# Taking the constant products out of TensorE's waits in a four-layer decoder kernel

## The reference

```python
x = x + _L0_attn_ref(_layernorm(x, axis=-1), ...)
x = x + _L0_xattn_ref(_layernorm(x, axis=-1), ctx_1024, ...)
x = x + _L0_ffn_ref(_layernorm(x, axis=-1), ...)
...
x = x + _L3_ffn_ref(_layernorm(x, axis=-1), ...)
```

## Time and profile before

| | |
|---|---|
| median of three runs | 1903.01 us |
| lowest and highest | 1902.84 and 1909.08 us |
| profiled execution | 1902.77 us |
| its span from first to last instruction | 1901.0 us |
| TensorE busy (matmul) | 1667.9 us, 88% |
| VectorE, ScalarE, GpSimd busy | 62%, 48%, 24% |
| mean granted TensorE clock | 0.952 of full |

### The profile page before, as it was taken

How to read it: one execution, slowest core, us unless ns; L and a number is a source line. 1 busy time by engine, 2 the same in 40 slices (tenths; PEclk the granted TensorE clock), 3 DMA queues, 4 the chain that set the end, 5 groups by cost and what they waited for, 6 DMA issues and landing times. The chain is left out here.

```text
span 1901.0 us, 37141 instructions
## 1 busy us (share of the span) xinstructions
PE 1667.9 (88%) x13775; PEld 1293.5 (68%) x13778; DVE 1177.0 (62%) x2317; ACT 921.2 (48%) x1953; POOL 449.8 (24%) x501
## 2 busy tenths in 40 slices
PE   7978855789999799976878879999999988999898
PEld 4766733558888646643667647777777766888676
DVE  3676688656666612226545678888888865666622
ACT  2445576246666411111344456767676644555432
POOL 1020011023333032221300224545445530000200
PEclk9999977899999999998989989999999989999899
DMA  2020000300010172221000000101010112110000
GB/s 101 3 92 3 4 30 27 118 18 26 25 33 25 68 317 44 46 50 38 15 2 28 18 17 26 33 25 33 25 33 25 28 39 100 34 33 25 1 1 22
DMA packets 27679, 77.58 MB, mean 41 GB/s; under 512 B 2992, under 2 KB 14896, under 8 KB 25392
## 3 DMA queue, kind: packets, MB, share of 16 engines
q1 hardware_dynamic: 23488, 70.91, 10.9%
q0 software_dynamic: 4080, 5.13, 1.7%
HBM read 62.75 MB, written 13.28 MB: 40 GB/s over the span
## 5 line engine op out<-in xcount | busy, mean ns | idle before, releaser
L2575 DVE SCALAR_TENSOR_TENSOR arena<-bank,arena 128x508 f32<-128x508 f32 (+2 forms) x204 | 151.5, 743 | 27.9 <-ACT arena L2571 15.6
L2701 PE MATMUL bank<-L3a_wo,L3a_y_gated 128*128 128x256 f32 x512 | 124.0, 386 | 0.0
L2930 DVE TENSOR_TENSOR L3a_decays<-L3a_decays,L3a_cb_masked 128x512 f32<-128x512 f32 x128 | 94.7, 802 | 43.4 <-ACT L3a_decays L2813 43.4
L225 PE MATMUL bank<-const 128*128 128x512 f32 (+1 forms) x156 | 79.6, 644 | 42.5 <-PEq L65 42.5
L2813 ACT ACTIVATE L3a_decays<-bank 128x512 f32<-128x512 f32 x128 | 66.1, 602 | 97.0 <-PE bank L2675 97.0
L2728 PE MATMUL bank<-L3a_xnT_high,L3a_w_high 128*128 128x512 f32 x256 | 105.8, 413 | 1.5 <-ACT L3a_decays L2813 1.5
L2701 PEld LDWEIGHTS bank<-L3a_wo,L3a_y_gated 128*128 128x128 f32 x512 | 92.4, 190 | 17.6 <-issue 7.3
L2728 PE MATMUL bank<-L3a_xnT_high,L3a_w_low 128*128 128x512 f32 x256 | 99.8, 390 | 0.0
L2728 PE MATMUL bank<-L3a_xnT_low,L3a_w_high 128*128 128x512 f32 x256 | 99.7, 389 | 0.0
L1932 PE MATMUL bank<-L1f_experts,xnT 128*128 x184 | 84.6, 604 | 0.9 <-DVE xnT L2035 0.7
L3027 POOL TENSOR_TENSOR arena<-arena 128x1024 f32<-128x1024 f32 x32 | 81.3, 2541 | 14.7 <-ACT arena L2820 14.7
(11 more groups left out here) (612 smaller groups left out, 4641.2 us busy)
## 6 DMA issues: line engine op xcount, KB each, us to landing
arena<-in_L3p SPq DMA_DIRECT2D x32, 388.0 KB, 3.0
L1f_experts<-in_L1f SPq DMA_DIRECT2D x8, 1536.0 KB, 19.7
arena<-in_L1x SPq DMA_DIRECT2D x18, 384.0 KB, 3.0
arena<-in_L3x SPq DMA_DIRECT2D x18, 384.0 KB, 3.0
arena<-in_L0f SPq DMA_DIRECT2D x1, 4224.0 KB, 13.2
arena<-in_L3f SPq DMA_DIRECT2D x1, 4055.0 KB, 12.3
rows_sent<-L1a_blank SPq DMA_DIRECT2D x1, 2967.0 KB, 11.2
xnT<-rows_sent SPq DMA_DIRECT2D x23, 129.0 KB, 2.0
```

The costliest lines, as they stand in the source:

```text
L225: self.nc.tensor.matmul(self.k.ps[bank][:, 0:width], self.k.ident, self.k.const[:, 0:width], start=True, stop=True)
L2575: return nc.vector.scalar_tensor_tensor(dst[:, :, d:], psum[:, :, 0:P - d], wcol, dst[:, :, d:], ALU.mult, ALU.add)
L2701: mm = nc.tensor.matmul(ps[g // 2][:, (g % 2) * C:(g % 2 + 1) * C], yg[:, o, g * P:(g + 1) * P], wo[:, o, :], start=False, stop=False, ski ...
L2930: nc.vector.tensor_tensor(d, d, cbm[:, 4 * half:4 * half + 4, :].rearrange("p b t -> p (b t)"), ALU.mult).then_inc(S["dec_ready"], 1)
```

## The change

All calls of `idle` and the function itself are removed; the waits, the transposes and all other instructions stay as they are.

```diff
-    def idle(self, pe, n, width=HALF, bank=7):
-
-        for _ in range(n):
-            self.nc.tensor.matmul(self.k.ps[bank][:, 0:width], self.k.ident, self.k.const[:, 0:width], start=True,
-                                  stop=True)
-
     def tensor(self, pe):
         nc, k = self.nc, self.k
-        if self.busy:
-            self.idle(pe, 2)
         for h in range(2):
             for j in range(4):
                 b = 4 * h + j
                 by_dve = b in self.BY_DVE
-                if self.busy and b in ((1, 2) if self.measured else (1, 2, 3, 5, 6, 7)):
-                    self.idle(pe, 1, C)
                 pe.wait_ge(self.s_xn[by_dve], (self.BY_DVE if by_dve else self.BY_ACT).index(b) + 1)
...
                 r.matmuls(gate_w)
-                ln.idle(pe, 6, bank=6)
                 pe.wait_ge(s_both, 1)
...
                 mm.then_inc(s_prefix, 1)
-                ln.idle(pe, BUSY, bank=7)
                 pe.wait_ge(s_owner, 1)
```

More of the change, by code:

```diff
@@ L3514 @@
 CENTRED = 6 * C
-TILES, BUSY, ROW = 23, 28, C + 2
+TILES, ROW = 23, C + 2
 STAGES = [l0_attn, l0_xattn, l0_ffn, l1_attn, l1_xattn, l1_ffn, l2_attn, l2_xattn, l2_ffn, l3_attn, l3_xattn, l3_ffn]
```

## The result

| | before | changed |
|---|---|---|
| median of 11 runs each | 1904.04 us | 1912.97 us |
| lowest to highest | 1900.01 to 1909.08 us | 1908.9 to 1916.76 us |
| span of the profiled execution | 1901.0 us | 1908.3 us |
| mean granted clock | 0.952 | 0.929 |

The account below looks back on a forecast made before the run. Most stages were taken to run at TensorE's pace (88% busy). Earlier transposes -3.8, dense matmuls +10.4, narrow +9.6, router +0.4 gave +16.6 us; less 4 us for spared places, +12.6 us: 1915.5 us, range 1899 to 1926 us.

Parts of the forecast that it names:

- within 0.5%: Whole kernel: time within 0.5%, 9.5 us, of the kernel before, chance 0.40; slower than that got 0.56.
- hidden or half paid: Rival, chance 0.35: later waits absorb late first matmuls, or the low clock lasts 2 us, not 4; +6.6 us, 1909 us.
- Price of the low clock: Stage starts at 1.2 GHz: 32 narrow matmuls cost 3.2 us more, 16 transposes take 3.4 us, dense matmuls cost double.
- Term 4: Router of l1_ffn: prefix sums start 1.9 us earlier, run 1.8 us slower, first expert tile loses 0.5 us; +0.4 us.
- two places in ten are spared: Ten stage starts: transposes alone raise the clock in two, taking 4 us off, from +16.6 to +12.6 us.
- terms 2 and 3: Stage starts: first matmuls run at 1.2 GHz, dense ones costing +10.4 us and narrow ones +9.6 us.
- Term 3: l1_ffn, l2_ffn and l3_attn: 32 narrow first matmuls at 1.2 GHz cost 3.2 us each stage, +9.6 us.
- the low clock feeds on itself: Rival, chance 0.12: after narrow matmuls the clock stays at 1.2 GHz for denser ones; three places at 3 us more, 1924 us.
- The clock at 1.00 at the first matmul in most stages: Sign at the stage starts that the prediction is wrong and the kernel gets faster instead.
- the faster case: Rival, chance 0.06: constants are mostly delay, transposes raise the clock in nearly every stage; about -10 us, 1893 us.
- The gap interrupts it, so I let it start anew: Stage starts: the 0.7 us copy gap restarts the clock's rise; 4 us at 1.2 GHz from first matmul, 2 us lost.
- The mean clock: Sign over the whole kernel: mean granted clock falls from 0.952 to about 0.94, some 35 us more at the low level.

Follow-up runs that it names:

- router_out: Kernel before without only the 34 router constants in l1_ffn, the stage starts keeping theirs: 1904.01 us against 1904.19, ratio 0.9998.
- combined: Kernel before with start constants kept in three stages, one product at other starts, one in the gaps, none at the router: 1902.44 us against 1901.12, ratio 1.0002.
- the second profile: The changed kernel run once more, unaltered, for another trace: one execution, 1914.79 us, on a chip where the kernel before has a median of 1901.12 us.
- gap_filled: Changed kernel plus one 256-column constant product behind the last transpose in nine stages: 1907.65 us against 1904.19 for the kernel before, ratio 1.0004.
- front_filled: Changed kernel plus one 256-column constant product ahead of the first transpose in nine stages: 1914.4 us against 1904.84 for the kernel before, ratio 1.0046.
- l3a_out: Kernel before without the constants in l3_attn alone: 1905.95 us against 1904.84, ratio 1.0009.

## Why the prediction was right, and where it was off

The sign held, and the mechanism in part: the kernel is slower because the clock is at 1.2 GHz behind some stage starts, but in fewer of them than forecast, at a higher price in two, and in one (`l2_ffn`) not at the first matmul. The chip gave +8.9 us where the forecast was +12.5 us, so the time came out inside the range, and by the prediction's own bound it lies on the side called "within 0.5%" (0.47%), to which 0.40 was given and not 0.56. The rival "hidden or half paid", +6.6 us, is nearer to it than the forecast.

- *Price of the low clock.* 32 narrow matmuls: forecast 3.60 + 3.2 = 6.8 us, measured 6.88 us. Sixteen transposes: forecast 3.4 us and 0.4 to drain, measured 3.81 us; the first matmul 0.3 us earlier in `l2_attn`, measured, from ScalarE's root, 5.92 us in place of 6.21, 0.3 us. For `l3_ffn` forecast 1.4 us earlier, measured 5.80 in place of 7.30, 1.5 us. These prices were right.
- *Term 4.* The prefix sums gained 1.8 us and lost 1.9 us to the clock. Forecast +0.4 us, and `router_out` measured nothing to tell from it.
- *The step that was off* is "two places in ten are spared". In the changed kernel's trace the clock was up at the first matmul in six of the ten starts: in `l1_xattn`, for about 1 us, as forecast, and in `l0_attn`, `l1_ffn`, `l2_attn`, `l2_ffn` and `l3_ffn`, for which terms 2 and 3 had 12.4 us in all. Taking these off by the prediction's own prices leaves +4.2 us. The profiles differ by 7.4 us because, for the most part, other entries were too small: `l1_attn` and `l3_attn` cost 7.9 us and not 5.7, `l1_ffn` and `l2_ffn` together 2.7 us and not -0.2. That these errors offset each other to land inside the range is partly luck.
- *Term 3 was too large in two of its three stages.* It priced the 32 narrow matmuls at 0.2 us each in all three. In `l1_ffn` and `l2_ffn` they started at 2.4 GHz and the clock fell on the way, 4.81 and 4.73 us in place of 3.71, about 1 us more each and not 3.2; only in `l3_attn` was it 3.3 us. There, too, the narrow matmuls left the clock low and the dense ones behind them began at 1.2 GHz (4.43 us in all). That is the case called "the low clock feeds on itself", in one stage. `l2_ffn` before, then changed:

```profile
1044.46 3.71 PE L302 MATMUL bank<-arena,xnT 128*128 128x6 f32 x32 [0.72 <-ACT xnT L219]
...
1046.89 4.73 PE L292 MATMUL bank<-arena,xnT 128*128 128x6 f32 x32 [0.72 <-ACT xnT L219]
```

- *A sign that misled.* "The clock at 1.00 at the first matmul in most stages" was to mean the faster case. It came, six in ten, and the kernel is slower all the same: two stages at 0.50 outweigh the rest.
- *Hidden lateness.* `l2_xattn` was not spared, yet lost 0.33 us, not 1.7. Three traces in which the clock fell 0.9 us ahead of its first transpose separate this from luck: it stayed low for 3.4 us in the kernel before, 6.8 us in `combined` and 10.2 us in the changed kernel, and the stage took 118.20, 118.20 and 118.53 us. So the low clock is taken up later in the stage; which wait takes it up I did not look for. (Where the clock fell at another moment, as in the second profile, the stage is 2.0 to 2.5 us shorter.)
- *The gap.* "The gap interrupts it, so I let it start anew" was an assumption. `gap_filled` against `front_filled` shows for the total (1.0004 against 1.0046), and the traces with a like fall show in four stages, that the open gap keeps the clock low longer. It did not always: in `l2_attn` of the changed kernel and `l3_attn` of `l3a_out` the clock rose in spite of it.
- *The Trainium skill's rule* that transposes do not engage the full clock (TensorE: Matmul & The Clock Gate, Part 4) does not hold here. In `l2_attn` of the changed kernel and in `l3_attn` of `l3a_out` the clock rose after nothing but sixteen float32 transposes, 4.1 and 4.5 us behind the first of them.
- *The mean clock* was to be a sign: the mean granted clock should fall to about 0.94. It fell to 0.929: the traces have 88 us more at the low level, not 35. `l1_ffn`, with the router's long wait, accounts for 38 us of that, which I had not counted and which cost next to nothing. The mean clock is no measure of the loss.

**What stays open.** What makes the clock fall 0.8 us or 2.3 us ahead of a stage's transposes was not controlled; it moved between kernels that have the same instructions in the stage, and between two executions of one kernel. So it is shown for four stages that a product in the gap shortens the low stretch when the clock falls at a given moment, and for the whole that it saves time, but not that it saves time in each stage. Whether other places or widths would beat the kernel before was tried in three versions, none of which did.

## What to carry to other kernels

Constant products are worth what the next real work would lose at the low clock, less what they delay: the place to try first is where TensorE would idle between the last short work and the first long one, rather than in front of work that is about to be ready. Here one of 256 columns in a gap of 0.7 us did most of what four or eight at a start did, the same one ahead of the transposes did nothing, and 34 around a wait of 30 us did nothing; no placement beat the original. And compare stage by stage over several profiles, and only between those in which the clock fell at the same moment: with that moment a stage can swing by 2 to 4 us.

## What the runs showed of the hardware that I had not expected

- The same sixteen transposes followed by the same 0.69 us of idling brought the clock to 1.00 ahead of the first matmul in one execution and left it at 0.50 for 4.3 us longer in another (`l2_attn` of the changed kernel, 4.1 and 8.4 us behind the first transpose).
- Behind the open gap, 32 matmuls of 64 columns did not bring the clock back: without a gap between them they ran 6.88 us at 1.2 GHz throughout, and likewise in three more traces of `l3_attn`, while at 2.4 GHz the same 32 ran 3.60 us without losing it. With the product in the gap the clock rose 1.5 us into them.
- TensorE was busy 40 us less and the kernel took 9 us longer, with the other engines' busy times unchanged to 2.1 us.
